# Order of the third q/k product, the P turns and the second-stage maximum within a step

## What is computed

```
h  = cond(x, w1[idx1]) + b[idx1]                 # [B, C, T]
q, k, v = h @ Wq.T, h @ Wk.T, h @ Wv.T           # 16 heads of 32
P  = softmax(q k^T / sqrt(32) + alibi, causal)
x1 = x + (P v) @ Wo.T
g  = cond2(x1, w2[idx2])
act_quant(y) = clip(round(y * s), -127, 127) / s,  s = 127 / max(|y|) per token
u  = relu(act_quant(fwht(g)) @ ternary(w_up).T) ** 2
out = x1 + act_quant(fwht(u)) @ ternary(w_down).T
```

## Time and profile before

| | us |
|---|---|
| runs | 760.9, 761.53, 762.89 (median 761.53) |
| profiled execution, its own time | 763.7 |
| span of its profile | 761.9 |
| PE busy / PEld busy | 727.9 (96%) / 616.3 (81%) |
| DVE busy | 668.4 (88%) |
| ACT busy | 421.9 (55%) |
| POOL busy | 214.3 (28%) |
| mean granted TensorE clock | 0.982 |

### The profile page before, as it was taken

One profiled execution on the slowest core, in us unless ns is written; L12 is line 12 of the kernel. 1 busy time (PEld: TensorE's weight loads), 2 busy tenths in 40 slices (PEclk: granted clock), 3 DMA queues, 4 the chain that ended last, 5 costly groups with the idle time before them and its releaser, 6 DMA issues.

```text
span 761.9 us, 23166 instructions
## 1 busy us (share of the span) xinstructions
PE 727.9 (96%) x9637; PEld 616.3 (81%) x9671; DVE 668.4 (88%) x1346; ACT 421.9 (55%) x844; POOL 214.3 (28%) x228
## 2 busy tenths in 40 slices
PE   7888999999999999999999999999999999997777
PEld 4777888888888888888888888888888888886643
DVE  3596999999999999999999999999999999988866
ACT  2478566556565565556565565565665665564421
POOL 1123333222333333222333332223333332122300
PEclk9899999999999999999999999999999999998979
DMA  7651111011111111111111110111111010110000
GB/s 235 226 182 37 37 50 41 28 34 52 49 51 50 51 49 27 40 36 51 50 50 51 51 45 23 35 49 50 50 51 50 31 31 31 30 31 16 6 11 28
DMA packets 37422, 39.91 MB, mean 52 GB/s; under 512 B 21189, under 2 KB 21317, under 8 KB 37317
## 3 DMA queue, kind: packets, MB, share of 16 engines
q1 hardware_dynamic: 34180, 32.04, 13.7%
q10 hardware_dynamic: 3136, 6.39, 2.4%
HBM read 30.02 MB, written 8.39 MB: 50 GB/s over the span
## 4 chain that ended last, share of the span: by engine, by line
PE 83%; DVE 8%; ACT 3%; POOL 2%; DMA 2%; issue 1%; SPq 1%; ACTq 0%; DVEq 0%
PE bank L367 43%; PE bank L499 8%; PE bank L535 7%; PE bank L391 4%; PE bank L357 4%; PE bank L481 4%; PE bank L508 4%; PE bank L437 4%; PE bank L454 3%; POOL gT L264 2%; DMA v_kd<-in_L_attn_Wv_dram 2%; PE bank L489 1%; DVE hid L264 1%; PE bank L519 1%; DVE hid L982 1%
## 5 line engine op out<-in xcount | busy, mean ns | idle before, releaser
L264 POOL TENSOR_TENSOR gT<-gT 128x256 f32<-128x256 f32 x124 | 107.2, 884 | 454.7 <-ACT gT L696 452.3
L264 DVE TENSOR_TENSOR hid<-hid 128x512 f32<-128x512 f32 x128 | 100.7, 828 | 0.0
L671 ACT ACTIVATE v_kd<-bank 64x256 f32<-64x256 f32 x128 | 48.5, 379 | 73.6 <-PE bank L367 72.5
L367 PE MATMUL bank<-h_hi,wk_hi 128*128 128x256 f32 x252 | 74.5, 296 | 5.6 <-ACT kT L660 5.6
L367 PE MATMUL bank<-h_hi,wq_hi 128*128 128x256 f32 x256 | 75.0, 293 | 0.0
L367 PE MATMUL bank<-h_lo,wq_hi 128*128 128x256 f32 x256 | 72.6, 284 | 0.0
L367 PE MATMUL bank<-h_hi,wq_lo 128*128 128x256 f32 x256 | 72.6, 283 | 0.0
L367 PE MATMUL bank<-h_hi,wk_lo 128*128 128x256 f32 x252 | 72.0, 286 | 0.0
L367 PE MATMUL bank<-h_lo,wk_hi 128*128 128x256 f32 x252 | 71.9, 285 | 0.0
L707 ACT ACTIVATE late<-bank 128x512 f32<-128x512 f32 x64 | 37.6, 588 | 60.3 <-PE bank L499 60.2
L1124 POOL TENSOR_TENSOR s<-s,srow 128x512 f32<-128x512 f32 x64 | 66.6, 1044 | 11.2 <-DVE srow L885 11.2
(11 more groups left out here) (126 smaller groups left out, 1946.9 us busy)
## 6 DMA issues: line engine op xcount, KB each, us to landing
x_in<-in_x_dram SPq DMA_DIRECT2D x32, 256.0 KB, 2.6
x_res<-in_x_dram SPq DMA_DIRECT2D x32, 256.0 KB, 3.4
out_dram<-late SPq DMA_DIRECT2D x32, 256.0 KB, 3.4
w_in<-in_L_cond_weights_dram SPq DMA_DIRECT2D x126, 16.0 KB, 2.4
bias_in<-in_fside_8xS_dram SPq DMA_DIRECT2D x62, 32.0 KB, 3.2
k_bd<-in_L_attn_Wk_dram ACTq DMA_DIRECT2D x1, 1024.0 KB, 5.4
s<-in_L_attn_Wq_dram ACTq DMA_DIRECT2D x1, 1024.0 KB, 6.7
v_kd<-in_L_attn_Wv_dram ACTq DMA_DIRECT2D x1, 1024.0 KB, 11.9
```

The costliest lines, as they stand in the source:

```text
L264: eng.tensor_tensor(dv[:, :, n], sv[:, :, 0], sv[:, :, 1], op).then_inc(done, 1)
L367: mm = pe.matmul(dst, lhs(a, k), rhs(b, k), start=(k == 0 and n == 0), stop=(k == KC - 1 and n == 2))
L671: ins = act.activation(v_kd[b * T:b * T + T, c % 4, e], blocks[e * T:e * T + T, :, b, :], ACT.Copy)
```

## The change

TensorE: `qk(c, 2)` comes directly behind `qk(c, 1)`; `turn_max(c - 2)` comes next, ahead of `hadamard1(c - 1)`; then the two halves of `turn_p` follow one another. A filler group of step 33 moves with it. ScalarE: the copy of `qk(c, 2)` moves up behind that of `qk(c, 1)`, ahead of `copy_hi`, `spread_k`, `copy_pt(c, 0)` and `scale_y1`. VectorE: the two chains are no longer interleaved; the whole chain of pair `c - 2` comes first, then that of pair `c - 1`. No instruction is added or removed and no wait is changed.

```diff
@@ TensorE
                 if next_group(c):
                     qk(c, 1)
+                if next_group(c):
+                    qk(c, 2)
                 if c == 1:
                     w_total(1)
                 if c == NPAIR:
                     keep_clock(12, up_w[:, 0, :])
+                if c == NPAIR + 1:
+                    keep_clock(22, up_w[:, 0, :])
+                if pair(c - 2):
+                    turn_max(c - 2)
                 if pair(c - 1):
                     hadamard1(c - 1)
-                if c == NPAIR + 1:
-                    keep_clock(22, up_w[:, 0, :])
-                if pair(c - 2):
-                    turn_max(c - 2)
                 if pair(c):
                     turn_p(c, 0)
-                if next_group(c):
-                    qk(c, 2)
-                if pair(c):
                     turn_p(c, 1)
@@ ScalarE
                 if c == 1:
                     w_round(1, 0)
+                if next_group(c):
+                    copy_next_qk(c, 2)
                 if pair(c + AHEAD):
                     copy_hi(c + AHEAD)
...
                 if pair(c - 1):
                     scale_y1(c - 1)
-                if next_group(c):
-                    copy_next_qk(c, 2)
                 if pair(c):
                     copy_pt(c, 1)
@@ VectorE
+                if pair(c - 2):
+                    max2(c - 2)
+                    limit2(c - 2)
+                    invert2(c - 2)
+                    scale2(c - 2)
+                    back2(c - 2)
                 if pair(c - 1):
                     max1(c - 1)
-                if pair(c - 2):
-                    max2(c - 2)
-                if pair(c - 1):
                     limit1(c - 1)
-                if pair(c - 2):
-                    limit2(c - 2)
-                if pair(c - 1):
                     invert1(c - 1)
-                if pair(c - 2):
-                    invert2(c - 2)
-                if pair(c - 1):
                     scale1(c - 1)
-                if pair(c - 2):
-                    scale2(c - 2)
-                if pair(c - 2):
-                    back2(c - 2)
-                if pair(c - 1):
                     back1(c - 1)
```

More of the change, by code:

```diff
@@ L614, in _ @@
                     keep_clock(12, up_w[:, 0, :])
-                if pair(c - 1):
-                    hadamard1(c - 1)
                 if c == NPAIR + 1:
@@ L620, in _ @@
                     turn_max(c - 2)
+                if pair(c - 1):
+                    hadamard1(c - 1)
                 if pair(c):
                     turn_p(c, 0)
-                if next_group(c):
-                    qk(c, 2)
-                if pair(c):
                     turn_p(c, 1)
```

## The result

| | before | after |
|---|---|---|
| median of four runs, us | 762.21 | 789.83 |
| lowest, highest | 760.9, 764.68 | 787.46, 791.64 |
| profiled execution, its own time | 763.7 | 791.64 |
| its span | 761.9 | 789.8 |
| mean granted TensorE clock | 0.982 | 0.974 |

The ratio after to before is 1.0351 with an interval from 1.032 to 1.0382: 24 to 29 us slower. The profiled execution is the slowest of the four; the other spans are 785.7 to 789.2 at clocks of 0.976 to 0.987.

What follows compares the result with a forecast made beforehand. TensorE was taken as saturated in the steady steps, so new waits add fully: 26 x 0.80 = 20.8, plus 0.8 for steps 28 and 29 and 2.9 at the end, 24.5 us on 761.53, giving 786; range 776 to 794.

Steps and rivals of the forecast that it cites:

- both waits: Likeliest case: TensorE waits for V's copy and again ahead of pv; 0.80 us a steady step, 786 us, chance 0.76.
- Part 1: TensorE, qk(c, 2) directly behind qk(c, 1): it must wait for V to be copied out, 0.43 us a step.
- Part 2: ScalarE queues behind the copy of qk(c, 2): about 1.35 us idle, pv 0.67 us late a step, 0.43 included.
- Part 3: VectorE's chains in turn: scale_y1 waits for scale1, adding 0.2 us; pv 0.84 to 0.9 late, 0.80 taken.
- The sign named for this part: On ScalarE, scale_y1 would show idle time ended by line 913; if not, the step is nearer 0.67.
- Part 4: TensorE's edge waits at hadamard1 and turn_max, up to 0.08 and 0.04 us a step, go; gain worth nothing.
- Steps 0 and 1 are set by loading and rounding weights; 0: In the first two steps the change was counted as costing 0 us.
- The last steps: Steps 28 and 29 cost 0.8 us; steps 30, 31 and 32 cost 0.5, 1.3 and 1.1; 33 and 34 nothing.
- the V wait alone: Rival: only qk(c, 2)'s wait for V binds; 28 x 0.43 = 12.0 us plus 2.9, 776.5 us; chance 0.12.
- The one that was not slower: Rival: V is up in time, edge waits pace TensorE; gain at most 3.1 us against 2.9, 761; chance 0.04.
- The clock rival: Rival: new TensorE gaps put one piece a step at 1.2 GHz; 24.7 us more, 811 us; chance 0.06.

Runs made afterwards that it cites:

- experiment 7: The changed kernel with two of the four activations of V's copy left out (output wrong); 775.11 us, ratio 1.0169 to the kernel before.
- experiment 1: The changed kernel with hadamard1 ahead of turn_max again and the VectorE chains interleaved again; 801.25 us, ratio 1.0491 to the kernel before.
- experiment 2: The kernel before with turn_max ahead of hadamard1 and the VectorE chains one after the other, no q/k product moved; 790.81 us, ratio 1.0377.
- ninth kernel: The kernel before with nine filler matmuls ahead of hadamard1 in steps 30 and 31; 761.63 us, ratio 0.9984 to the kernel before.

## Why the prediction was right

The forecast of 786 missed the median of 789.83 by 3.8 us, inside its range; the likeliest case, both waits, is the one that happened. The miss is smaller than its parts, and that is luck: the steady steps were taken 1.8 us too dear, and the first and last steps 4.3 us too cheap.

- **Part 1, the wait for V: right.** 0.43 us a step predicted, 0.46 measured in experiment 7. PE's load follows V's copy by 0.06 (0.05 taken). On weight loads taken ahead: this one did not start before the wait ended, although no load had been done for 0.41 us, so in this kernel nothing of the restart is hidden that way.
- **Part 2, ScalarE's queue: right.** Predicted were 1.35 us of idle time and `pv` 0.67 us late by this path alone; measured 1.38, and 7.13 - 6.43 = 0.70 by the first load of `pv`. By its first matmul it is 7.17 - 6.43 = 0.74, and that is the whole 0.73 of the step; `pv` itself is as long as before (0.85 and 0.86 us).
- **Part 3, the VectorE chain: mis-sized.** Predicted ready 414.04 - 408.01 = 6.03 us behind the start of V's copy, measured 5.81, and ScalarE got there at 5.85. The chain adds nothing; it is level with ScalarE's queue. The first half of the sum was exact: `max1` starts 427.19 - 422.63 = 4.56 behind V's copy, 412.58 - 408.01 = 4.57 predicted. The 0.2 is in the second half: from `max1` to `scale1` it is 1.10 us and not 1.25, and `scale1` takes 0.15 and not 0.21. I had put the lengths of the other chain's small operations (0.21) where this chain has 0.15. The sign named for this part, idle time of `scale_y1` ended by `scale1`, is absent. I took 0.80 a step for 0.73, 26 x 0.07 = 1.8 us too much. But what I had called a cost is also a gain: experiment 1 shows that with `turn_max` and the chains in their old order the step would be 0.64 longer, at `spread_scale`. I had checked what comes late behind `pv`, and never asked what the two chains did for `spread_scale`.
- **Part 4, nothing gained from the waits at the edge: right.** Line 481 doesn't wait any more and nothing became faster.
- **"Steps 0 and 1 are set by loading and rounding weights; 0": this step failed.** Measured 2.9. `w_total(1)` is a moved instruction that I did not count: in the diff its lines don't move, the product moves past them. The rounding that I thought to be the cover waits for exactly this instruction.
- **The last steps.** 0.8 for steps 28 and 29 was right (0.69). 2.9 for steps 30 to 32 was too small, 4.3 measured: from V of step 30 to V of step 31 0.3, from there to the copy behind `pv` of step 31 1.7 (8.42 became 10.10, predicted 1.3), and 2.3 after it (predicted 1.1). On the chain `hadamard1` took 1.71 us in each of steps 30 to 32, at a granted clock of 0.50 (1.05 was counted for step 32), and in step 33 `down` took 2.51 us instead of 1.68. That the longer wait ahead of it, 4.4 us for 2.6, is what lowered the clock isn't shown: in experiment 2 waits of 4.4, 4.4 and 4.1 us were followed by `hadamard1` of 1.37, 1.92 and 1.06 us, at granted clocks of 0.73, 0.50 and 1.00.

Of the rivals, the V wait alone would have given 776.5 and is ruled out by the 32 waits of line 454 and by experiment 7. The one that was not slower needed V to be up in time, and the 30 waits of line 367 say that it was not; experiment 2 adds that the column maximum, one of its two edge waits, is no sooner there when asked for sooner. The clock rival did not occur in the steady steps (PEclk 1.00), but the lower clock is part of what made step 1 (0.87 instead of 1.00) and steps 32 and 33 dearer than I said.

## What to carry to other kernels

If the profile shows an engine saturated, take each wait of the moved instruction and find the end of what it waits for; the distance between that and the new place is the price, once for every step. Then look for what the moved instruction's consumers are queued with: here half as much again came from a copy that a second engine did in program order. When a block moves past a line that the diff leaves unmarked, that line has moved too. And where two paths arrive together, an experiment that shortens one of them and shows no change has found the second, not cleared the first.

## What the runs showed of the hardware

After standing 2.8 us for P in step 1, TensorE ran `scores` and `up` at nearly twice and 1.6 times their usual length, at a granted clock of 0.55, with a cost of 1.0 us outside the wait itself. With the waits of 0.20 and 0.32 us in each steady step the granted clock stayed at 1.00 throughout. The same wait is not always followed by the same clock: of the three waits of 4.1 to 4.4 us at the end of experiment 2 one was followed by `hadamard1` at 0.50, one at 0.73 and one at 1.00. And filler matmuls put into the waits of the kernel before came with a `hadamard1` of step 31 of 1.16 us at a granted clock of 1.00, where the trace before has 1.92 us at 0.55 (timeline of the ninth kernel, the first set alone):

```profile
710.97 1.16 PE L481 MATMUL bank<-cst_sb,gT 128*128 128x128 f32 x8 [0.61 <-POOL gT L264]
```
